# Layer norms on ScalarE, and a residual that starts the sum in PSUM

## What is computed

```python
rkv = x @ W_rkv + b_rkv;  r, k, v = split(rkv)
r = sigmoid(r);  k = exp(k);  kv = k * v
u1, u2 = scan over time of (kv, k) with decay lam      # y[t] = lam * y[t-1] + u[t]
a = (u1 + gamma * kv) / (u2 + gamma * k + 1e-06) * r
z = layernorm(x + a @ W_o + b_o)
xr = mu_r * z + (1 - mu_r) * z_prev;  xk likewise with mu_k    # z_prev: one token earlier
k2 = square(relu(xk @ W_k))
out = layernorm(z + sigmoid(xr @ W_r) * (k2 @ W_v))
```

## Time and profile before

| | |
|---|---|
| median of 3 runs | 2763.93 us (2758.83 to 2767.05) |
| span of the profiled execution, first to last instruction | 2760.2 us |
| TensorE busy | 2582.5 us, 94% |
| VectorE busy | 2410.0 us, 87% |
| ScalarE busy | 1112.7 us, 40% |
| GpSimd busy | 1227.9 us, 44% |
| DMA, mean over the span | 40 GB/s |

### The profile page before, as it was taken

How to read it: one execution, slowest core, us unless ns; L and a number is a source line. 1 busy time by engine, 2 the same in 40 slices (tenths; PEclk the granted TensorE clock), 3 DMA queues, 4 the chain that set the end, 5 groups by cost and what they waited for, 6 DMA issues and landing times.

```text
span 2760.2 us, 36072 instructions
## 1 busy us (share of the span) xinstructions
PE 2582.5 (94%) x12800; PEld 2185.4 (79%) x12800; DVE 2410.0 (87%) x3275; ACT 1112.7 (40%) x1935; POOL 1227.9 (44%) x779
## 2 busy tenths in 40 slices
PE   7899999999999999999999999999999999999997
PEld 5678887778887788877888877887788877788886
DVE  8898898888898888998889989889888899898884
ACT  4334343434443343443434443434434343434343
POOL 3444444444443444544444434445344444444453
PEclk9999999999999999999999999999999999999998
DMA  4011011011011110100111101101001111011000
GB/s 164 8 39 47 31 47 35 27 48 47 31 42 36 33 47 31 47 31 32 47 35 42 39 24 46 46 31 47 31 31 46 31 48 39 24 46 47 31 31 24
DMA packets 57806, 110.94 MB, mean 40 GB/s; under 512 B 7040, under 2 KB 7040, under 8 KB 57088
## 3 DMA queue, kind: packets, MB, share of 16 engines
q1 hardware_dynamic: 57600, 108.31, 11.8%
HBM read 74.73 MB, written 33.55 MB: 39 GB/s over the span
## 4 chain that ended last, share of the span: by engine, by line
PE 48%; DVE 24%; issue 16%; POOL 8%; ACT 2%; DMA 1%; SPq 0%; DVEq 0%; POOLq 0%; ACTq 0%
PE bankB L792 7%; PE bankB L790 7%; PE bankB L791 7%; PE bankA L773 5%; PE bankA L774 5%; PE bankA L775 5%; PE bankB L838 5%; PE bankB L840 4%; PE bankB L839 4%; DVE xk_f L662 3%; DVE att_f L616 3%; POOL rstd L317 3%; POOL att_f L308 3%; DVE key L601 3%; DVE xr_f L662 3%
## 5 line engine op out<-in xcount | busy, mean ns | idle before, releaser
L773 PE MATMUL bankA<-x_hi,wrkv_hi 128*128 128x512 f32 x1536 | 611.0, 398 | 81.5 <-DVE kv L595 58.4
L774 PE MATMUL bankA<-x_lo,wrkv_hi 128*128 128x512 f32 x1536 | 603.4, 393 | 0.0
L775 PE MATMUL bankA<-x_hi,wrkv_lo 128*128 128x512 f32 x1536 | 602.6, 392 | 0.0
L308 POOL TENSOR_TENSOR att_f<-att_f,gate 128x512 f32<-128x512 f32 x128 | 204.7, 1599 | 594.3 <-DVE att_f L621 594.3
L608 DVE RECIPROCAL gate<-gate 128x512 f32<-128x512 f32 x128 | 429.2, 3353 | 4.4
L773 PEld LDWEIGHTS bankA<-x_hi,wrkv_hi 128*128 128x128 f32 x1536 | 291.4, 190 | 154.9 <-DVE kv L595 71.9
L838 PE MATMUL bankB<-xk_hi,wk_hi 128*128 128x256 f32 x1024 | 305.7, 298 | 69.4 <-ACT zT L438 67.4
L775 PEld LDWEIGHTS bankA<-x_hi,wrkv_lo 128*128 128x128 f32 x1536 | 291.2, 190 | 62.2
L774 PEld LDWEIGHTS bankA<-x_lo,wrkv_hi 128*128 128x128 f32 x1536 | 291.7, 190 | 56.4
L417 ACT ACTIVATE key<-bankA,b_sb 128x512 f32<-128x512 f32 x128 | 86.6, 676 | 562.6 <-PE bankA L775 550.3
L330 POOL TENSOR_TENSOR t<-t,y 128x512 f32<-128x512 f32 x128 | 191.5, 1517 | 257.2 <-DVE t L682 257.2
(11 more groups left out here) (84 smaller groups left out, 6020.0 us busy)
## 6 DMA issues: line engine op xcount, KB each, us to landing
x_f<-in_xT SPq DMA_DIRECT2D x128, 256.0 KB, 3.9
y<-in_x SPq DMA_DIRECT2D x128, 256.0 KB, 2.7
out<-t SPq DMA_DIRECT2D x128, 256.0 KB, 2.0
wrkv_f<-in_w_rkv SPq DMA_DIRECT2D x3, 768.0 KB, 6.8
wo_f<-in_w_o SPq DMA_DIRECT2D x1, 1024.0 KB, 10.2
wr_f<-in_w_r SPq DMA_DIRECT2D x1, 1024.0 KB, 12.0
wk_f<-in_w_k SPq DMA_DIRECT2D x1, 1024.0 KB, 13.9
wv_f<-in_w_v SPq DMA_DIRECT2D x1, 1024.0 KB, 15.8
```

Of the source, the lines that this page charges most:

```text
L308: pool.tensor_tensor(att_f[:, c], att_f[:, c], gate[:, c % 2], ALU.mult).then_inc(att_made, 1)
L773: pe.matmul(bank[:], w_hi, x_hi[:, h], start=(h == 0), stop=False)
L774: pe.matmul(bank[:], w_hi, x_lo[:, h], start=False, stop=False)
L775: last = pe.matmul(bank[:], w_lo, x_hi[:, h], start=False, stop=(h == NC - 1))
```

## The change

- `normalise` moves from VectorE to ScalarE: one Identity activation per tile, with `rstd` as scale and `shift` = -mean * rstd as bias. For the first layer norm it reads the PSUM bank and writes z to y; for the second it works on t in place.
- `inverse_std` on GpSimd does more: it adds epsilon, negates the mean (0 - mean), takes the power and multiplies, four instructions of 128x2 instead of one; the last waits for the two ahead of it.
- `bias_rows` (GpSimd) and `attention_rows` (VectorE) are gone. A new `begin_sum` on VectorE writes y + bo into the bank of the output product before it, and the product adds onto it (no `start`). Statistics read the bank. The bank is released by z (`z_made`) instead of the sum.
- The previous column is kept by ScalarE, in `mixed_high`.
- Before the first step four matmuls write the four banks of `bankB` once (`columns_written`).

The core of the diff; in the `step` functions only the order moves, and the rows below show it:

```diff
             def inverse_std(s, which, half):
+                tiles = slice(HT * half, HT * half + HT)
+                wait(pool, ln_mean[which], s.count(NT, HT * half + HT))
+                pool.tensor_tensor(ve[:, which, tiles], mv[:, which, tiles, 1], eps_ln[:], ALU.add)\
+                    .then_inc(ln_var[which], 1)
+                pool.tensor_tensor(shift[:, which, tiles], zero[:, 0:HT, 0], mv[:, which, tiles, 0], ALU.subtract)\
+                    .then_inc(ln_negated[which], 1)
                 wait(pool, ln_var[which], s.count(NH, half + 1))
-                tiles = slice(HT * half, HT * half + HT)
                 pool.tensor_tensor(rstd[:, which, tiles], ve[:, which, tiles], half_pow[:], ALU.pow)\
                     .then_inc(ln_rstd[which], 1)
+                wait(pool, ln_negated[which], s.count(NH, half + 1))
+                wait(pool, ln_rstd[which], s.count(NH, half + 1))
+                pool.tensor_tensor(shift[:, which, tiles], shift[:, which, tiles], rstd[:, which, tiles], ALU.mult)\
+                    .then_inc(ln_shift[which], 1)
...
+            def normalise(s, which, half, source, rows, done):
+                wait(act, ln_shift[which], s.count(NH, half + 1))
+                for i in range(HT):
+                    tile = HT * half + i
+                    act.activation(rows(tile), source(tile), ACT.Identity, bias=shift[:, which, tile:tile + 1],
+                                   scale=rstd[:, which, tile:tile + 1]).then_inc(done, 1)
...
+                if half == NH - 1 and s.back(-1).first_of_batch():
+                    act.activation(zT[:, :, 0:1], zero[:], ACT.Copy).then_inc(s_col0, 1)
+                else:
+                    act.activation(zT[:, :, 0:1], zT[:, :, HALF:HALF + 1], ACT.Copy).then_inc(s_col0, 1)
...
+            def begin_sum(s, half, run):
+                for tile in range(HT * half, HT * half + HT):
+                    wait(dve, y_loaded[tile], s.count(16, 16))
+                    if s.batch is None and s.s == 0 and tile == 0:
+                        dve.wait_ge(s_bo, 16)
+                    bank_free(dve, run, "WO", tile)
+                    if s.batch is None and s.s == 0:
+                        dve.wait_ge(columns_written, NBANK)
+                    dve.tensor_tensor(psum_of("WO", tile)[:], y[:, y_slot(s, tile)], bo[:], ALU.add)\
+                        .then_inc(sum_begun, 1)
...
             def attention_out(s, half, run):
                 for tile in range(HT * half, HT * half + HT):
-                    bank_free(run, "WO", tile)
+                    wait(pe, sum_begun, s.count(NT, tile + 1))
...
-                    rows_product(s, "WO", tile, att_hi, att_lo, tile * P, wo_hi, wo_lo)
+                    rows_product(s, "WO", tile, att_hi, att_lo, tile * P, wo_hi, wo_lo, begun=True)
```

More of the change, by code:

```diff
@@ L771, in project @@
                         wait(pe, x_lo_made, s.count(NC, h + 1))
+                        if s.batch is None and s.s == 0:
+                            pe.matmul(bankB[h][:], wrkv_hi[:, c, which, h], x_hi[:, h], start=True, stop=True)\
+                                .then_inc(columns_written, 1)
                     w_hi, w_lo = wrkv_hi[:, c, which, h], wrkv_lo[:, c, which, h]
@@ L820, in receptance @@
                 for i in range(HT):
-                    bank_free(run, "R", HT * half + i)
+                    bank_free(pe, run, "R", HT * half + i)
                     wait(pe, xr_lo_made, s.count(NH, half + 1))
```

140 lines of the change are left out of this document (66 added, 74 removed).

## The result

The changed kernel takes **2713.22 us** (median of 4 runs, 2711.5 to 2716.13); the kernel before took 2762.02 beside it. The ratio is 0.9816, 95% interval 0.98 to 0.9832.

What follows compares the result with a forecast made beforehand. TensorE (94% busy) was held by waits on one ScalarE/VectorE chain. Span 2760.2 - 31.5 (30 steps of -2.15 + 1.1) - 3 + 7 = 2732.7; median 3.7 above: 2736 us, own range 2715 to 2757, 8 in 10 2670 to 2805.

Steps and rivals of the forecast that it cites:

- Stall A: TensorE's wait in each step for kv from VectorE, at a projection; costs 1.7 us, predicted to go.
- Stall B: TensorE's wait before the keys for ScalarE's zT copy; predicted to stay at 2.1 us, keys 2.15 us earlier.
- Why the scan comes earlier: VectorE's scan of chunk 1: predicted 3.2 us earlier, at 1032.35 instead of 1035.53, though ScalarE is 2.7 later.
- Stall C: New wait at the step's end, value product for ka_lo behind ScalarE's t normalisation: 1.1 us, bounds 0.3 and 2.6.
- the second rival: Tiny GpSimd instructions cost as much as the power, step-end wait about 2.4 us, slower: 2790 us; chance 0.18.
- slow key stretches: First 48 key products after the zT wait, partly at 1.2 GHz: 7.33 us instead of 5.76 in 18 of 30 steps.
- "Costed at nothing": Bias and residual added in the output product's bank: adds come early enough, no cost to the step.
- Start and end: Outside the steps: first step's longer kv wait gives some 3 us; last block's adds behind ka_lo cost 7.
- The first (both stalls go): Rival: scale not held up by xr_lo, keys on time, slow clock gone too: 2646 us; chance 0.17.
- The third: Rival: GpSimd's att_lo gets ahead of VectorE's scan (margin 0.2 us), step at +1.25: 2805 us; chance 0.13.

Runs made afterwards that it cites:

- a_low_split: Changed kernel with xr_lo and xk_lo of the first half (GpSimd) each in four instructions of 256 columns instead of one of 1024: 2675.76 us.
- b_column: Kernel before with only the copy (or zeroing) of the previous column moved from VectorE to ScalarE: 2760.07 us, ratio 0.9983 to before.
- a_column_back: Changed kernel with only the previous-column copy put back on VectorE, between the mix and the scan: 2714.16 us.
- a_norms_back: Changed kernel with all four normalisation pairs back on VectorE in the old order, the rest of the change kept: 2775.76 us, ratio 1.0044 to before.
- a_tail_pair_late: Changed kernel with ScalarE's t pair at the step's end placed behind the tanh and key squares instead of ahead: 2696.95 us.
- a_chain_first: Changed kernel with ScalarE's zT copies and scaled copies first, the z and t pairs moved behind xr_hi and xk_hi: 2639.18 us.
- a_scan_late: Changed kernel with one 256-column statistics instruction into a scratch tile put on VectorE ahead of chunk 1's scan: 2824.5 us, ratio 1.0222 to before.
- a_residual_back: Changed kernel with bias adds again on GpSimd at the step's end and VectorE adding them behind the output product; norms stay on ScalarE: 2698.07 us.
- a_both_residual_back: Changed kernel with ScalarE's pairs moved back at step start and end, and bias adds on GpSimd, added on VectorE behind the output product: 2647.85 us.
- a_both_tail: Changed kernel with ScalarE's pairs moved back at step start and end, and the last step's final ka_lo behind the last block's first adds: 2598.28 us.

## Why the prediction was right, and where it was off

- **Stall A goes.** Right: its stretch is 2.03 shorter, where 1.7 was reckoned. The path was right in time too: the scan starts 7.4 us after the zT copies are released, 7.55 were worked out.
- **Stall B stays at 2.1, behind the scale held up by xr_lo.** Right: the scale takes 2.77 (a_low_split shows that it is the cause), and the keys start 22.0 us after that point, 22.1 expected. The wait is 1.7 to 2.0.
- **Why the scan comes earlier** was told wrong in one part. The prediction took the 2.40 us of the column copy as a cost that goes. b_column and a_column_back show that it was GpSimd's time in VectorE's row. The sum came out because the mix was reckoned from ScalarE alone, at its unhindered pace. In the kernel before, GpSimd's att_f and att_lo held up the two halves of the mix, by 1.0 each:

```profile
1027.98 2.71 DVE L662 SCALAR_TENSOR_TENSOR xr_f<-zT,vecs,xr_f 128x256 f32<-128x256 f32 x4
1030.60 2.70 DVE L662 SCALAR_TENSOR_TENSOR xk_f<-zT,vecs,xk_f 128x256 f32<-128x256 f32 x4
```

```profile
1028.14 1.46 POOL L308 TENSOR_TENSOR att_f<-att_f,gate 128x512 f32<-128x512 f32 x1 [3.23 <-DVE att_f L621]
1030.35 1.48 POOL L312 TENSOR_TENSOR att_lo<-att_f,att_hi 128x512 fp32r<-128x512 f32 x1 [0.75 <-ACT att_hi L430]
```

  From the release to the mix it took 3.2 there and takes 4.2 now; 2.0 in the mix and 2.3 at the copy are gone: 3.3 net, of which the prediction had 3.2. Three hits go together. att_f is now done before the mix, and the mix then keeps 0.44 us behind ScalarE's last scaled copy, so that att_lo, whose att_hi (0.63) stands behind these copies on ScalarE, comes 0.16 after the scan's start. The prediction placed att_lo in the new schedule and not att_f; a_norms_back shows the mix hit when att_f falls into it. That it lay clear of the mix was not reckoned, and there the sum was lucky.
- **Stall C.** The mechanism was right: ScalarE's t pair waits for GpSimd's shift, ka_lo and the value product for it. The size, 1.1, is 1.07 where it happens, but it happens in 23 steps. In the others a pause at the loop boundary comes first. The mean is 0.90 a step. The tiny GpSimd instructions took 0.20 (0.25 reckoned), so the second rival fell. The pairs on ScalarE took 1.32 (from PSUM) and 1.41 (from SBUF) from their start to the next instruction's, which is what the prediction had reckoned at 1.36 and 1.44; the durations in the rows, 1.45 and 1.52, overlap the next instruction.

```profile
974.33 0.20 POOL L332 TENSOR_TENSOR ve<-mv,eps_ln 128x2 f32<-128x2 f32 x1
974.48 0.20 POOL L334 TENSOR_TENSOR shift<-zero,mv 128x2 f32<-128x2 f32 x1
974.63 0.70 POOL L337 TENSOR_TENSOR rstd<-ve,half_pow 128x2 f32<-128x2 f32 x1
975.48 0.20 POOL L341 TENSOR_TENSOR shift<-shift,rstd 128x2 f32<-128x2 f32 x1
975.71 1.52 ACT L470 ACTIVATE t<-t,shift,rstd 128x512 f32<-128x512 f32 x2 [2.70 <-POOL shift L341]
```

- **The term that was missed: the clock.** The sum let the slow key stretches stand as they were, since stall B stays. It shortened by 0.3 us only, and 11 of 17 went: -0.55 a step, 16 us, most of the 23. Of the rest, stalls A and B gave 0.2 a step more than reckoned and stall C cost 0.2 less, while the output product cost 0.19. Why so many slow stretches went is open: a_tail_pair_late has 14 of them behind the same waits.
- **"Costed at nothing" for the sum in the bank** was not quite so: 0.19 a step on the output product, all of it in four steps behind a loop boundary. Start and end were right, -2.8 (3) and +7.6 (7).
- **The rivals.** The first (both stalls go) needed the scale ahead of xr_lo. The change as made doesn't give it, and a_chain_first does (2639.2, where the rival said 2646). The third is the state of a_scan_late.

What stays open: what decides, besides its length, whether a pause of 1.9 us is followed by the lower clock; the traces show the outcome (6, 6, 5 and 14 of 29 in the changed kernel, a_residual_back, a_column_back and a_tail_pair_late), and not the cause. What the norms would cost on VectorE behind the numerator is open too.

## What to carry to other kernels

Where GpSimd works beside VectorE's two-tensor instructions, an instruction's duration in the trace is not its price: look at which GpSimd instruction ran beside it, and expect the hit to pass to the next instruction when this one is taken away. By the rows, taking work off VectorE paid in this change by moving it against GpSimd, so read from the two timelines who asks first, and by how much, before and after. When work goes to an engine with room, queue it behind what the next stage waits for: moving three pairs that nobody near waits for further back on ScalarE was worth another 109 us, more than twice the change itself.

## What the runs showed of the hardware

- Two engines 0.16 us apart: in one order the pair of instructions costs VectorE nothing, in the other 1.0 us. Where they ask at the same moment (a_both_residual_back, 23 steps) the order differs from step to step, 15 to 8, so one kernel has steps of 78.8 and of 83.0 us. Its runs spread by 17 us (2641.81 to 2658.79), where a_both_tail's spread by 2.
- Not only two-tensor instructions of VectorE are hit. In the kernel before, the column copy took 0.16 to 2.41 us and a normalisation, which reads one tensor, 0.54 to 1.52 (two beside the bias adds 2.95). The reciprocal (3.35 to 3.36) and the statistics (0.67 to 0.69) never changed.
- A subtraction of 128x2 on GpSimd takes 0.20 us, a power 0.70.
- An Identity of 128x512 with scale and bias from memory takes ScalarE 0.66 us from PSUM and 0.71 from SBUF, from start to start.
- A wait for zT of 1.7 to 2.0 us was followed by the 1.2 GHz level for a part of the next 48 products in 5 to 14 of 29 steps (four kernels); one of 2.2 to 2.4 us in 17 of 28 (the kernel before); one of 0.7 to 0.9 us in none of 29 (a_low_split); one of 4.1 to 4.3 us in all 29 (a_scan_late).
